# Last group of layer 1 moved behind layer 0 of the next batch, and batch 0 worked in half blocks with layer 1 following W1 block by block

## What is computed

```
x = x + (x @ W0.T + b0 + coeff[b] * (x @ (2*mask[b] - 1)))       # layer 0
x = x + (x @ W1.T + b1 + 2 * (x @ A[id[b]]) @ B[id[b]])          # layer 1, A 1024x16, B 16x1024
```

## Time and profile before

| | |
|---|---|
| median of 3 runs | 424.15 us (424.01 to 424.44) |
| the profiled execution's own time | 426.43 us |
| its span, first to last instruction | 424.6 us |
| PE matmul busy | 389.6 us (92%) |
| DVE / ACT / POOL busy | 228.5 / 158.8 / 46.1 us |
| mean granted clock of PE | 0.972 of full |
| read from HBM, written | 52.97 MB, 8.39 MB |

### The profile page before, as it was taken

One profiled execution on the slowest core, in us unless ns is written; L12 is line 12 of the kernel. 1 busy time (PEld: TensorE's weight loads), 2 busy tenths in 40 slices (PEclk: granted clock), 3 DMA queues, 4 the chain that ended last, 5 costly groups with the idle time before them and its releaser, 6 DMA issues.

```text
span 424.6 us, 6715 instructions
## 1 busy us (share of the span) xinstructions
PE 389.6 (92%) x2782; PEld 385.9 (91%) x2782; DVE 228.5 (54%) x265; ACT 158.8 (37%) x282; POOL 46.1 (11%) x43
## 2 busy tenths in 40 slices
PE   5986049999999999999999999999999999999997
PEld 5986049999999999999999999999999999999996
DVE  1788747752584727752474717843475717843300
ACT  2433715341544325341444324341444324432311
POOL 1338340020002000020001100020000100020000
PEclk9799659999999999999999999999999999999999
DMA  8985780665047520665046520675036520520011
GB/s 270 398 271 182 250 277 4 229 220 175 2 145 210 194 78 2 213 234 181 0 137 220 190 82 0 203 243 181 2 129 211 206 82 2 198 100 2 0 51 49
DMA packets 21220, 61.80 MB, mean 146 GB/s; under 512 B 3012, under 2 KB 4292, under 8 KB 21190
## 3 DMA queue, kind: packets, MB, share of 16 engines
q1 hardware_dynamic: 18304, 52.96, 38.2%
q10 hardware_dynamic: 2886, 8.41, 4.9%
HBM read 52.97 MB, written 8.39 MB: 144 GB/s over the span
## 4 chain that ended last, share of the span: by engine, by line
PE 83%; DMA 8%; DVE 3%; issue 2%; ACT 2%; POOL 1%; SPq 1%; ACTq 0%; DVEq 0%
PE z_ps L290 44%; PE y_ps L258 25%; PE y_ps L267 11%; DMA ring<-in_mask 4%; DMA ring<-in_w 2%; PE z_ps L311 2%; DMA w_t<-in_w 2%; ACT y_two L357 1%; DVE wc_lo L470 1%; POOL ring L237 1%; DVE w_lo L481 1%; DVE y_two L493 1%; ACT w_hi L345 1%; PE t_ps L303 0%; DVE ring L463 0%
## 5 line engine op out<-in xcount | busy, mean ns | idle before, releaser
L290 PE MATMUL z_ps<-w_hi,y_two 128*128 128x344 f32 (+1 forms) x768 | 191.5, 325 | 23.2 <-DVE w_lo L481 17.4
L290 PEld LDWEIGHTS z_ps<-w_hi,y_two 128*128 128x128 f32 x768 | 136.4, 190 | 25.2 <-DVE w_lo L481 17.6
L258 PE MATMUL y_ps<-x_two,wc_hi 128*128 128x256 f32 x1024 | 135.1, 285 | 2.7 <-ACT wc_hi L338 2.7
L258 PEld LDWEIGHTS y_ps<-x_two,wc_hi 128*128 128x128 f32 x1024 | 129.5, 194 | 3.0 <-DVE x_two L486 3.0
L290 PE MATMUL z_ps<-w_lo,y_two 128*128 128x344 f32 (+1 forms) x384 | 124.3, 324 | 0.0
L470 DVE SCALAR_TENSOR_TENSOR wc_lo<-ring,coeff_neg,wc_hi 128x1024 fp32r<-128x1024 f32 x64 | 91.5, 1432 | 51.3 <-ACT wc_hi L338 51.0
L338 ACT ACTIVATE wc_hi<-ring,coeff_neg 128x1024 fp32r<-128x1024 f32 x64 | 73.6, 1151 | 69.7 <-PE y_ps L267 41.4
L463 DVE SCALAR_TENSOR_TENSOR ring<-ring,coeff_two,w_t 128x1024 f32<-128x1024 int32 x64 | 82.0, 1290 | 6.5 <-DMA ring<-in_mask 6.4
L267 PE MATMUL y_ps<-x_two,wc_lo 128*128 128x256 f32 x512 | 73.2, 286 | 4.7 <-DVE wc_lo L470 4.7
L290 PEld LDWEIGHTS z_ps<-w_lo,y_two 128*128 128x128 f32 x384 | 73.1, 190 | 0.0
L267 PEld LDWEIGHTS y_ps<-x_two,wc_lo 128*128 128x128 f32 x512 | 66.7, 194 | 5.8 <-DVE wc_lo L470 5.8
(11 more groups left out here) (25 smaller groups left out, 74.0 us busy)
## 6 DMA issues: line engine op xcount, KB each, us to landing
ring<-in_mask SPq DMA_DIRECT2D x64, 512.0 KB, 3.6
x_raw<-in_x SPq DMA_DIRECT2D x32, 256.0 KB, 5.8
out<-z_rows ACTq DMA_DIRECT2D x14, 512.0 KB, 5.0
w_t<-in_w SPq DMA_DIRECT2D x8, 512.0 KB, 7.3
ring<-in_w SPq DMA_DIRECT2D x8, 512.0 KB, 4.3
b_raw<-in_lora_b SPq DMA_DIRECT2D x32, 64.0 KB, 2.6
out<-z_rows ACTq DMA_DIRECT2D x2, 340.0 KB, 2.2
a_raw<-in_lora_a SPq DMA_DIRECT2D x8, 64.0 KB, 2.8
```

The lines of the kernel that those rows point to most:

```text
L258: pe.matmul(ys, w, x_two[:, k, n, :], start=(k == 0 and o % PAIR == 0 and n == 0), stop=False, skip_group_check=True)
L290: ins = pe.matmul(z_ps[g][:, 0:EDGES[g + 1] - EDGES[g]], ys[:, k, s * P:(s + 1) * P], w[:, k, EDGES[g]:EDGES[g + 1]], start=(k == 0 and n ...
```

## The change

Four things are done.

- **Order of layer 1.** Group 2 of half 1 of batch b is no longer done at the end of `layer1(b)` but after `layer0(b+1)`, as `layer1_last(b)`. For batch 0, half 0 runs all three groups together, block k by block k (`layer1_first`); group 0 of half 1 then goes to bank `y_ps[3]` and comes before the groups of half 0 are closed.
- **Lora.** `lora_high` is cut in two: `lora_a_high(b)` once group 0 of half 1 of batch b-1 is closed, `lora_b_high(b)` once all of batch b-1 is closed. PE waits for `lora_lo_done` of 2b + 1 ahead of group 0 and 2(b + 1) ahead of closing it. The code of POOL's `lora_low` is the same as before.
- **Order on ACT and DVE.** From batch 1 on, `y_high` and `y_low` are followed by the conversion of x of the next batch, then the copy and store of the moved group, then the lora work. `h_low(b, 1)` comes after `step(b+1, 2)` instead of after `step(b+1, 1)`.
- **Batch 0.** Block 0 of W0 and of the mask is loaded in two halves, x group 0 on ACT's queue, and the other x groups one place later. W0(k) and mask(k) otherwise alternate as before. DVE, ACT and PE work in blocks of half the width, and DVE does both sums and both low parts of block k before it turns to k+1. SP loads four W1 blocks ahead of lora 0; the other four follow.

```diff
-            for k in range(KT):
-                load_w0(k)
-                load_mask(0, k)
-                if k % PAIR == 0:
-                    load_x(0, k // PAIR)
+            for k in range(1, KT):
+                load_w0(k)
+                load_mask(0, k)
+                if k % PAIR == 1 and k < KT - 1:
+                    load_x(0, k // PAIR + 1)
+            for k in range(RING):
+                load_w1(k)
             sp.wait_ge(ids_in, 16)
             load_lora(0)
-            for k in range(KT):
+            for k in range(RING, KT):
                 load_w1(k)
...
+            def layer1_first():
+                pe.wait_ge(lora_lo_done, 1)
+                for k in range(KT):
+                    pe.wait_ge(w1_lo_done, k + 1)
+                    pe.wait_ge(y_lo_done, k + 1)
+                    for g in range(NG):
+                        products(0, 0, g, k)
...
-                    if b == 0 and s == 0 and g == 0:
-                        pe.wait_ge(w1_lo_done, KT)
                     if s == 0 and g == 0:
-                        pe.wait_ge(lora_lo_done, 2 * (b + 1))
+                        pe.wait_ge(lora_lo_done, 2 * b + 1)
...
+            def layer1_last(b):
+                layer1_group(b, 1, 2)
+                close_group(b, 1, 2)
...
-            for b in range(NB):
-                layer0(b)
-                layer1(b)
+            layer0(0)
+            layer1(0)
+            for b in range(1, NB):
+                layer0(b)
+                layer1_last(b - 1)
+                layer1(b)
+            layer1_last(NB - 1)
...
-            def lora_high(b):
-                act.wait_ge(lora_in, 16 * 5 * (b + 1))
-                need(act, z_full, NG * ST * b)
-                act.activation(w1_hi[:, :, 0:R], a_raw[:], ACT.Copy).then_inc(lora_hi_done, 1)
+            def lora_a_high(b):
+                act.wait_ge(lora_in, 16 * 5 * (b + 1))
+                if b > 0:
+                    act.wait_ge(z_full, NG * (ST * b - 1) + 1)
+                act.activation(w1_hi[:, :, 0:R], a_raw[:], ACT.Copy).then_inc(lora_hi_done, 1)
+
+            def lora_b_high(b):
+                need(act, z_full, NG * ST * b)
                 act.activation(b_stack[0:LR, :], b_raw[0:LR, :], ACT.Copy).then_inc(lora_hi_done, 1)
...
-            for k in range(RING):
-                w1_high(k)
-            lora_high(0)
+            w1_high(0)
+            w1_high(1)
+            lora_a_high(0)
             act.wait_ge(b0_in, 16)
             for g in range(XG):
                 y_high(0, g)
-            for k in range(RING, KT):
+            for k in range(2, KT):
                 w1_high(k)
+            lora_b_high(0)
...
+                if a > 0:
+                    z_copy(a - 1, 1, 2)
+                    store(a - 1, 1)
+                    lora_b_high(a)
                 h_high(a, 0)
```

More of the change, by code:

```diff
@@ L125, in ring_filled, with parts @@
             eng.wait_ge(ring_in[e % RING], 16 * (e // RING + 1))
+        def parts(b, k, h=1):
+            return 2 * k + h + 1 if b == 0 else KT * (b + 1) + k + 1
         def block_read(eng, b, k):
@@ L136, in block_read, with z_bank @@
                 eng.wait_ge(block_used, (KT - 1) * b + k + 1)
+        def z_bank(b, s, g):
+            return y_ps[XG - 1] if (b, s, g) == (0, 1, 0) else z_ps[g]
         block = ctx.enter_context(nc.Block())
@@ L261, in layer0_low @@
             def layer0_low(b, k):
-                pe.wait_ge(wc_lo_done, KT * b + k + 1)
+                if b > 0:
+                    pe.wait_ge(wc_lo_done, parts(b, k))
                 for o in range(KT):
+                    if b == 0 and o % HT == 0:
+                        pe.wait_ge(wc_lo_done, parts(b, k, o // HT))
                     ys = y_ps[o // PAIR][:, (o % PAIR) * T:(o % PAIR + 1) * T]
@@ L288, in layer1_group @@
                         pe.wait_ge(y_lo_done, KT * b + k + 1)
[L289 to L295, removed]
+                    products(b, s, g, k)
             def turn_h(b, s):
@@ L428, in _ @@
                 h_high(a, 1)
-                weights_high(b, 2)
+                if b < NB:
+                    weights_high(b, 3)
                 h_copy(a, 1)
-                weights_high(b, 3)
                 z_copy(a, 1, 0)
                 z_copy(a, 1, 1)
[L434 to L440, removed]
@@ L442, in _ @@
-            a = NB - 1
-            for s in range(ST):
[L444 to L453, removed]
+                if b < NB:
+                    lora_a_high(b)
+                    for k in range(RING, KT):
+                        weights_high(b, k)
@@ L506, in _ @@
             dve.wait_ge(coeff_done, 2)
[L509 to L517, removed]
+            for k in range(KT):
+                weights_sum(0, k, 0)
+                if k % PAIR == 0:
+                    x_low(0, k // PAIR)
+                weights_sum(0, k, 1)
+                weights_low(0, k, 0)
+                weights_low(0, k, 1)
+            w1_low(0)
+            w1_low(1)
             dve.wait_ge(b0_in, 16)
@@ L525, in _ @@
                 a = b - 1
+                if a > 0:
+                    for g in range(XG):
+                        y_low(a, g)
+                for g in range(XG):
+                    x_low(b, g)
                 h_low(a, 0)
[L527 to L530, removed]
                 weights_sum(b, 0)
@@ L533, in _ @@
                 step(b, 1)
+                step(b, 2)
                 h_low(a, 1)
-                for k in range(2, KT):
+                for k in range(3, KT):
                     step(b, k)
-                for g in range(XG):
-                    y_low(b, g)
+            for g in range(XG):
+                y_low(NB - 1, g)
             for s in range(ST):
```

135 lines of the change are left out of this document (97 added, 38 removed).

## The result

The changed kernel takes 457.76 us (median of 4 runs, 457.55 to 457.87) against 424.29 us for the kernel before beside it (4 runs): a ratio of 1.078, interval 1.0753 to 1.0807. It is slower, by 33.5 us; forecast were +25.8 and 450.0, with 438 to 463 as the range. The span of the profiled execution went from 424.6 to 455.8 us (+31.2), its own time from 426.43 to 457.76 (+31.3). The rest of the 33.5 is that the execution profiled before stood 2.1 us over its own median, and the one after did not.

A forecast was written before the change was run, and what follows sets the result against it. Loading and splitting weights were taken to bound the kernel up to 59.13 us, then PE. Moved group +17.0, start -2.6, new order +4.4 and clock +7.0 gave +25.8: 450.0 us, range 438 to 463.

The forecast's parts named there:

- The moved group and the wait that takes its place: Ahead of layer 1, batches 1 to 7: PE's 0.82 us waits become lora gaps of 3.35 (last 2.65), +17.0 us.
- The clock: PE's clock falls in three of eight long gaps, at 2.34 us each: +7.0 us.
- rival 2: PE's clock falls in every gap, a repeated cold start: +37.5 us, 461.7 us, chance 0.17.
- the row of the 1.63 us idle at full clock: Evidence about 36 to 38 us: PE idle 1.63 of 2 us without its clock falling, cited for the clock holding.
- the fall 2.1 us into the first idle stretch: Evidence at 9.2 us: PE's clock fell 2.1 us after the warm-up ended, cited for it falling in every gap.
- The start: Layer 1 of batch 0 starts at 56.5 us instead of 59.13: -2.6 us, bounds -8 and +2.
- layer1_first does not follow block by block: Batch 0's layer 1: its first line waits for POOL's lora_lo_done, given only after the B operand; start at 56.5 us.
- Rival 3: Batch 0's layer 1 follows W1 block by block if POOL gives lora_lo_done early: 407.6 us, chance 0.03.
- New order in batch 0: Layer 1 of batch 0: 0.9 us for the copied bank and 3.5 at turning h, +4.4 us (bounds 0 and 7).
- The half blocks: Layer 0 of batch 0: halves and DVE's new order bring the last low part at 36 us instead of 39.56.
- The sum: Whole kernel: the terms add to +25.8 us, 452.2 against the profiled execution, 450.0 as median.

The follow-up runs named there:

- e1_split: The changed kernel, with POOL's low part of the lora A operand waiting for its own count, only the B part for both: 421.44 us, ratio 0.9916.
- e3_fill: The changed kernel, with 24 matmuls of unused result behind each moved group: 446.03 us, ratio 1.0487.
- e2_xlate: The changed kernel, with ACT's four x conversions behind the copy, store and lora B operand, POOL's wait kept: 454.02 us, ratio 1.0678.
- e6_both: e5_first plus the earlier split of h of half 1 of batch 0 from e4: 410.44 us, ratio 0.9653.
- e9_whole: e6_both with layer 0 of batch 0 in whole blocks and DVE's order as before the change: 410.12 us, ratio 0.9649.
- e5_first: e1_split, with POOL making batch 0's low lora A part between the identities of W1 blocks 3 and 4: 414.14 us, ratio 0.9738.
- e4: The changed kernel, with h of half 1 of batch 0 split earlier on ACT and DVE: 454.39 us, ratio 1.0685.
- e8: e6_both with lora 0 loaded ahead of all W1 blocks and POOL's b1 operations between W1 blocks 5 and 6: 408.01 us, ratio 0.9594.
- e11: e6_both with lora 0 loaded ahead of all W1 blocks and POOL's b1 operations behind W1 block 7: 407.44 us, ratio 0.9584.

## Why the prediction was right, and what it sized wrongly

- **The moved group and the wait that takes its place**: right, in mechanism and in place. The A part that PE needs was held by the B part through one shared count, and the B part by the moved group itself; e1_split removes only that and 36 us go. The gap was put at 3.35 us (2.65 ahead of batch 7) and is 3.0 (2.6), so the term of +17.0 measured +14.4. The error is in ACT's lateness for the copy: four conversions run in 2.08 us behind y, not 2.3, and the small wait into the copy is shared with them.
- **The clock**: the term that was mis-sized most. I took three of eight long stretches at 2.34 us, +7.0. The clock fell at all seven gaps, at 1.4 to 2.8 us each, not 2.34: +11.9, and e3_fill gives 11.9 for it too. It held behind the eighth stretch, the 2.8 us at the turning of h in batch 0 (granted clock 1.00 from 80.8 to 90.8 us). So rival 2's mechanism happened but for one stretch. Between the two ends, the row of the 1.63 us idle at full clock was the wrong neighbour; the fall 2.1 us into the first idle stretch was the near one. The length of a wait does not settle it alone: behind the same 2.8 us at the turning of h the clock held in e1_split as well, and fell in e2_xlate and e3_fill. The Trainium skill ("TensorE: Matmul & The Clock Gate", section "HAM oscillation — how this bites in real kernels") describes a loop whose recurring waits cost the cold start every time instead of once. The trace after agrees with that for the seven gaps, at 7.40 to 8.77 us for the first 36 matmuls against 5.96 before.
- **The start**: +0.3 instead of -2.6 (about -0.6 on the mean of the four profiles that share it). The chain named was right, step by step, up to y at 43.4 to 46.4 (forecast to end at 45.3): lora late behind W1 block 3, y behind lora, W1 blocks 6 and 7 late through that, and the B operand behind all of it. Two terms were short: the last low part ended at 37.7, not 36, though W1's last block was issued at 49.84, only 0.3 us behind the forecast; and this block took 6.3 us to land, not 4, which is most of the 2.9 us. Its row, and what follows, in the chain of the changed kernel:

```profile
49.84 6.29 DMA ring<-in_w
...
57.71 1.05 ACT b_stack L460
58.76 0.07 issue
58.83 0.56 POOL w_lo L236
```

  The forecast took the median of eight such loads. The last one took 4.96 us in the kernel before, 5.54 in e6_both and 4.88 in e9_whole, each time with the four x loads of the next batch issued right behind it, as here. Why it took 6.3 here stays open.
- **"layer1_first does not follow block by block"**: right, but the reason given was half of it. Rival 3 was said to turn on the shared count alone; e1_split splits the count, and layer1_first still waits, since POOL makes the A part behind all of W1. Only with POOL's list changed too (e5_first) does it follow the blocks.
- **New order in batch 0**: +4.4 forecast, +4.3 measured (2.8 at the turning of h and 0.6 for the copied bank, 3.4 of the 4.4 foreseen; 0.5 in the first 72 matmuls, 14.26 us where the same 72 took 8.09 + 1.89 + 3.77, since the clock came back 5.7 us behind their start and not 4.6; 0.4 not traced).
- **The half blocks**: I gave them, with the other order of DVE, some 2 us of earlier low parts. e9_whole undoes both, and its last low part ends at 36.7 us, before the 37.8 of e6_both: the two together give nothing. In the kernel before it ended at 39.6; what e9_whole keeps of the change ahead of that point is where the x loads stand, which was not tried by itself.
- **The sum**: against its own time 452.2 was forecast and 457.8 measured. The terms account for 5.1 of the 5.6: start +2.9, gaps -2.6, clock +4.9, new order -0.1. That the gaps came out shorter hid half of what the clock cost more: the time is nearer to the forecast than its terms are. The median was taken 2.3 below the profiled execution, as it stood before; after the change there is no such distance.

Rival 3 failed where it was said to decide, at the shared count. The time is 1.8 us above the forecast's own range of 445 to 456, and within 438 to 463, because rival 2 was inside it. Of the cases that were priced, rival 2 (461.7, chance 0.17) is the nearest in time and in mechanism.

## What to carry to other kernels

When work is moved to cover a wait, list what else the instruction behind it waits for, and follow each of those through every engine it passes: here one semaphore counted two operands, and the later one depended on the work just moved. A wait of 3 us on PE cost 4.7 us here, since the clock fell with it; where such a gap could not be removed, matmuls that nobody reads were cheaper than idling. Changes at a start bound by loads need the whole chain: six edits (e4 to e8 and e11) that each removed or shortened a visible wait gave from nothing to 7 us.

## What was not expected of the hardware

PE's clock fell to its lower level at gaps of 2.6 us between stretches of dense matmuls, in seven of seven (e2_xlate), and each cost 1.55 us more than the gap. In the kernel before it had held where PE was idle for 1.63 of 2 us. Behind one and the same wait of 2.8 us in batch 0 it held in two profiles (the change, e1_split) and fell in two (e2_xlate, e3_fill), so a single profile does not tell whether such a wait is safe.

Work on POOL over only two partitions held up DVE's two-input operations. Two low parts took 4.29 instead of 1.63 us and another 3.42 instead of 1.23, by about the length of POOL's operation beside them (2.69 and 2.34 us).
